# Loading odd and even image rows of the mixing stage as pairs, each pair by one 128-partition DMA

## The chip, the core and the metric

One core of a Trainium2 chip runs the whole kernel in one launch. The metric is the device time in microseconds (us). TensorE (PE), VectorE (DVE), ScalarE (ACT) and GpSimd (POOL) compute; SyncE (SP) issues loads; ACT issues the stores of this stage. All DMAs of the core are carried out by the same 16 DMA engines.

## The reference

Input x is 8 x 64 x 256 x 256 in f32 (batch, channel, row, column). Layer 0 normalizes x by groups, and then, for each batch,

```
y  = mlp1(x)                                   # 64 -> 192 channels, of which 128 are used
x1 = shift1(y[..., :64]);  x2 = shift2(y[..., 64:128])
out = bar0 * x1 + bar1 * x2                    # bar: one softmax weight pair per batch and channel
o  = mlp2(out) * sigmoid(bn(x)) * x
x  = x + o
```

shift1 and shift2 move a quarter of the channels each by one pixel down, up, right or left, with the edge repeated. Everything linear in a batch folds into four 64 x 64 matrices, one for each direction, so the mixing is a sum of four matrix products of shifted images. Layer 1 normalizes again, takes a two-dimensional real FFT, mixes 64 x 32 modes by complex weights, transforms back and adds.

## The kernel before, in words

The kernel runs in stages, one after the other: statistics of x, small matrices from them, the mixing stage (layer 0's output to a scratch tensor in DRAM), a second normalization, the forward transform, the mixing of modes, and the inverse transform. The change lies in the mixing stage and in the last step of the small matrices.

The mixing stage (lines 512 to 742) walks over 8 batches and, in each, over 16 tiles of 16 image rows (`MR`), 128 tiles in all. The loop is unrolled over two batches (`NI` = 32 tiles) and repeated four times. Tile n uses buffer n mod 4 (`NX` = 4) of the input `XT` (mix_x), of `XC` (centred) and of `G` (gated), and buffer n mod 2 of the output `XO` (mix_out) and of psum.

A buffer of `XT` holds, on partitions 0 to 63 (one per channel), the 17 rows from the row above the tile, one column to the right; on partitions 64 to 127, 17 rows from the tile's first row on, without that shift. So one 128-row matrix product reads two shifted images at once, and two such products (m = 0 and 1) make the four directions. Output rows of one parity go to psum partitions 0 to 63 and those of the other to 64 to 127 (`par`).

The steps of one tile, with the lines:

- SP waits until the convolution and the sigmoid of the tile that had the buffer before are done, then issues two loads (L565, L568), each of nine rows by 64 channels to 64 partitions; at the upper and lower image edge there is a third (L572, L574).
- DVE fills the other half of each partition range from the half that was loaded: `up` (L687) copies from the lower to the upper partitions, `down` (L692) from the upper to the lower.
- POOL copies the edge columns (`pad`, L590, two instructions) after `down`.
- PE runs the matrix products (L618) after the pads.
- ACT takes the tile's mean from it (L641) after the pads, in two halves on even tiles; on odd tiles DVE does one half (L700). Then comes the sigmoid (L649).
- DVE multiplies psum by the gate (L722), and then forms the output and its sum (L731).
- ACT issues the store to the scratch (L662) and sums the squares (L667).

Each engine has a written-out order in which work for tile n + 2 (loading step, copies, gate) stands between the steps of tile n; semaphores connect the engines. There is no planner. SP's queue holds nothing but the loads, in the order of the tiles.

In the stage before, DVE writes the folded matrices of all batches into `wall` (L503), four blocks of 64 x 64 per batch as `LAYOUT` says, one instruction for each.

Of the kernel before, what the change touches and what calls it, by code (L numbers as in the profile page):

```python
# [44 lines left out]
LAYOUT = ((0, 0, 2), (1, 0, 1), (0, 1, 0), (1, 1, 3))  # L45
PITCH = W + 1
# [67 lines left out]
def program(nc, x, w1m, b1m, w2m, b2m, sa1, sa2, gamma, beta, wr1, wi1, wr2, wi2, const, out):  # L114
    top = ExitStack()
    with top:
# [34 lines left out]
        wall = sb(top, "wall", [P, B + 1, P])  # L151
# [7 lines left out]
        with ph:  # L159
# [133 lines left out]
            with nc.Block() as block:  # L293
# [77 lines left out]
                def _(dve):  # L371
# [141 lines left out]
        with ph:  # L513
            NX = 4
            XT = [sb(ph, f"mix_x{i}", [P, MR + 1, PITCH]) for i in range(NX)]
# [4 lines left out]
            one = sb(ph, "one", [P, MR + 1])  # L520
            wcur = [sb(ph, f"wcur{i}", [P, P]) for i in range(2)]
            pcur = [sb(ph, f"pcur{i}", [P, 6]) for i in range(2)]
            loaded = [sem(f"mix_loaded{i}") for i in range(NX)]
            stored = [sem(f"mix_stored{i}") for i in range(2)]
            one_set = sem("mix_one_set")
            doubled, padded, batch_ready = sem("mix_doubled"), sem("mix_padded"), sem("mix_batch_ready")
# [4 lines left out]
            ITER = B // 2  # L531

            x1_par = x1.rearrange("b (r e) c w -> b (e c) r w", e=2)

            def split(n):

                return n % 2 == 1

            def loaded_by(i, n):

                q, t = n % NX, n % NB
                edge = 16 if q in (0, NX - 1) else 0
                batch = NB // NX * 32 + edge
                return i * (2 * batch) + n // NB * batch + (t // NX + 1) * 32 + (edge if q == 0 or t == NB - 1 else 0)
# [7 lines left out]
            with nc.Block() as block:  # L552
                @block.sync
                def _(sp):
                    with sp.Fori(0, ITER) as i:
                        for n in range(NI):
                            ch = bass.ds((i * 2 + n // NB) * C, C)
                            t, xt = n % NB, XT[n % NX]


                            sp.wait_ge(conv_done, i * NI + n + 1)
                            sp.wait_ge(sig_done, i * NI + n + 1)
# [8 lines left out]
                            if t == 0:  # L571
                                sp.dma_start(xt[0:C, 0:1, 1:W + 1], x_rows[ch, 0:1, :]).then_inc(loaded[n % NX], 16)  # L572
                            if t == NB - 1:
                                sp.dma_start(xt[C:P, MR:MR + 1, 0:W], x_rows[ch, H - 1:H, :]  # L574
                                             ).then_inc(loaded[n % NX], 16)

                    for k in range(2):
                        sp.wait_ge(stored[k], B * NB // 2 * 16 + 16)

                @block.gpsimd  # L580
                def _(pool):
                    nc.gpsimd.memset(one[:, :], 1.0).then_inc(one_set, 1)
                    pool.wait_ge(one_set, 1)

                    def pad(i, n):

                        pool.wait_ge(doubled, i * NI + n + 1)
                        for half, to, of in ((0, 0, 1), (1, W, W - 1)):
                            h = slice(half * C, (half + 1) * C)
                            last = nc.gpsimd.tensor_tensor(XT[n % NX][h, :, to], XT[n % NX][h, :, of],  # L590
                                                           one[h, :], ALU.mult)
                        last.then_inc(padded, 1)

                    pad(0, 0)
                    pad(0, 1)

                    def body(i, final):
                        for n in range(NI - 2 * final):
                            pad(i, n + 2)

                    iterations(pool, body)

                @block.tensor
                def _(pe):
                    pe.sem_inc(conv_done, NX)
                    with pe.Fori(0, ITER) as i:
                        for n in range(NI):
                            j, k = n // NB, n % 2
# [13 lines left out]
                            last.then_inc(conv_done, 1)  # L622

                @block.scalar
                def _(act):
# [5 lines left out]
                    def gate(i, n):  # L631

                        j = n // NB % 2
                        if n % NB == 0:
                            act.wait_ge(batch_ready, i * 2 + n // NB + 1)
                        act.wait_ge(padded, i * NI + n + 1)

                        act.wait_ge(o_done, i * NI + n + 1)
                        for half in range(1 if split(n) else 2):
                            h = slice(half * C, (half + 1) * C)  # L640
                            last = nc.scalar.activation(  # L641
                                XC[n % NX][h, :].rearrange("p (r w) -> p r w", w=W),
                                XT[n % NX][h, 1:MR:2, 1 - half:1 - half + W],
                                ACT.Identity, bias=pcur[j][h, 4:5])
                        last.then_inc(xc_done, 1)
                        act.wait_ge(xc_done, i * NI + n + 1)
                        if split(n):
                            act.wait_ge(xc_dve, i * NB + n // 2 + 1)
                        nc.scalar.activation(G[n % NX][:, :], XC[n % NX][:, :], ACT.Sigmoid,  # L649
                                             bias=pcur[j][:, 1:2], scale=pcur[j][:, 0:1]).then_inc(sig_done, 1)  # L650
# [22 lines left out]
                def _(dve):  # L673
# [9 lines left out]
                    def up(i, n):  # L683

                        dve.wait_ge(loaded[n % NX], loaded_by(i, n))
                        xt, h = XT[n % NX], MR // 2
                        nc.vector.tensor_copy(xt[C:P, 0:h, 0:W], xt[0:C, 1:h + 1, 1:W + 1])  # L687

                    def down(n):

                        xt, h = XT[n % NX], MR // 2
                        nc.vector.tensor_copy(xt[0:C, h + 1:MR + 1, 1:W + 1], xt[C:P, h:MR, 0:W]).then_inc(doubled, 1)  # L692

                    def centre(i, n):


                        j = n // NB % 2

                        dve.wait_ge(doubled, i * NI + n + 1)
                        nc.vector.tensor_scalar(XC[n % NX][C:P, :].rearrange("p (r w) -> p r w", w=W),  # L700
                                                XT[n % NX][C:P, 1:MR:2, 0:W],
                                                pcur[j][C:P, 4:5], None, ALU.add).then_inc(xc_dve, 1)
# [5 lines left out]
                    for n in range(2):  # L708
                        up(0, n)
                        down(n)  # L710
                    centre(0, 1)

                    def body(i, final):
                        for n in range(NI):
                            j, k = n // NB, n % 2
                            ahead = not (final and n + 2 >= NI)
                            if ahead:
                                up(i, n + 2)
# [6 lines left out]
                            if ahead:  # L725
                                down(n + 2)
# [9 lines left out]
                            if ahead and split(n + 2):  # L736
                                centre(i, n + 2)
# [615 lines left out]
```

## Time and profile before

| | us |
|---|---|
| median of 3 runs | 3149.35 (3144.79 to 3153.17) |
| the profiled execution, its own time | 3155.57 |
| its span in the profile | 3153.8 |

Over the span PE is busy 71%, DVE 64%, ACT 41% and POOL 24%. The stages lie one after another, so these shares are averages over stages with different limits. The mean granted TensorE clock is 0.924 of full speed. A busy time is time in which an engine has an instruction in work; the "DMA share" is the mean busy time of the 16 DMA engines' packets, which overlap a little, so that it can be above 1. "idle before, releaser" in a group says how long the engine waited ahead of it and what ended most of the wait.

### The profile page before, as it was taken

To read this page: it belongs to the slowest core of one execution; us is meant where nothing else is said; L and a number is where in the kernel's file an instruction comes from. 1 tells how busy PE (TensorE), PEld (TensorE's weight loads), DVE (VectorE), ACT (ScalarE), POOL (GpSimd) and SP (SyncE) were. 2 spreads that over 40 slices of the span, in tenths; PEclk is the share of its full clock that TensorE was granted. 3 is DMA by queue.
4 is the path that set the end of the run, shared out by engine and by line. 5 is a ranking of instruction groups with operands and counts; after the bars stand their busy time and mean duration, and the time that the engine had idled before them with its cause. 6 is when DMAs were issued, how large, how long until landed. Compare 5 with 4: busy or idle time off the path is not lost. (4 is left out here: it accounts for less than half of the span.)

```text
span 3153.8 us, 39097 instructions
## 1 busy us (share of the span) xinstructions
PE 2252.6 (71%) x12960; PEld 1081.7 (34%) x12960; DVE 2027.7 (64%) x2317; ACT 1298.2 (41%) x1470; POOL 756.3 (24%) x477
## 2 busy tenths in 40 slices
PE   0000289888989888885999999945554898988784
PEld 0000123223323232331455444425553444444442
DVE  8999689989999999996665565620000454544442
ACT  1111078878887888885332232310000222212220
POOL 1000022332233322332655455500000111111112
PEclk9999999999999999998999999977787999998987
DMA  9999199999999999997877666669998999999999
GB/s 400 429 429 429 36 248 265 271 248 275 270 272 256 270 274 270 269 267 233 316 261 266 241 242 247 232 145 295 304 305 231 384 401 380 394 380 408 389 378 351
DMA packets 537808, 942.87 MB, mean 299 GB/s; under 512 B 16896, under 2 KB 459952, under 8 KB 493136
## 3 DMA queue, kind: packets, MB, share of 16 engines
q1 hardware_dynamic: 299264, 613.33, 61.9%
q10 hardware_dynamic: 202880, 192.95, 20.1%
q0 software_dynamic: 35536, 134.84, 11.2%
q8 instruction: 85, 1.39, 0.2%
q14 instruction: 43, 0.35, 0.0%
HBM read 647.46 MB, written 293.60 MB: 298 GB/s over the span
## 5 line engine op out<-in xcount | busy, mean ns | idle before, releaser
L618 PE MATMUL psum<-mix_x,wcur 128*64 128x512 f32 x4096 | 937.6, 614 | 150.3 <-POOL mix_x L590 134.3
L618 PEld LDWEIGHTS psum<-mix_x,wcur 128*64 128x64 f32 x4096 | 316.6, 139 | 770.8 <-issue 566.4
L1259 PE MATMUL psum<-tab_irow_icol_sign,inv_t 128*128 128x512 f32 x1024 | 495.8, 608 | 18.9 <-DVE inv_x L1306 16.0
L590 POOL TENSOR_TENSOR mix_x<-mix_x,one 64x17 f32<-64x17 f32 x256 | 323.2, 1262 | 747.6 <-DVE mix_x L692 740.2
L641 ACT ACTIVATE centred<-mix_x,pcur 64x2048 f32<-64x2048 f32 x192 | 384.2, 2001 | 204.1 <-POOL mix_x L590 188.9
L1077 POOL TENSOR_TENSOR fwd_diff<-x_tile 128x2048 f32<-128x2048 f32 x64 | 307.9, 4812 | 291.7 <-PE psum L869 256.5
L983 ACT ACTIVATE fwd_rows<-psum 128x512 f32<-128x512 f32 x256 | 152.2, 597 | 412.8 <-PE psum L869 387.9
L263 DVE BATCH_NORM_STATS2 stats<-stat_x 128x512 f32 x512 | 310.0, 678 | 17.5 <-DMA stat_x<-x 14.7
L731 DVE SCALAR_TENSOR_TENSOR mix_out<-gated,centred 128x2048 f32<-128x2048 f32 x128 | 293.6, 2294 | 41.3 <-issue 35.5
L722 DVE SCALAR_TENSOR_TENSOR gated<-psum,pcur,gated 128x2048 f32<-128x2048 f32 x128 | 300.9, 2351 | 16.3 <-PE psum L618 14.4
L1052 DVE COPY fwd_cols<-psum 128x136 f32<-128x136 f32 x512 | 154.6, 394 | 234.2 <-PE psum L880 233.2
L869 PE MATMUL psum<-fwd_sum,tab_ident_frow_fcol 128*64 128x512 f32 x512 | 282.3, 635 | 30.1 <-POOL fwd_diff L1077 20.3
L1287 ACT ACTIVATE inv_t<-psum 128x256 f32<-128x256 f32 x256 | 98.1, 383 | 478.5 <-PE psum L1250 478.5
L1122 PE MATMUL psum<-mode_w,mode_x 128*16 128x64 f32 x4096 | 169.9, 360 | 162.5 <-DMA mode_x<-modes_in 159.8
L869 PE MATMUL psum<-fwd_diff,tab_ident_frow_fcol 128*64 128x512 f32 x512 | 282.7, 636 | 0.0
L649 ACT ACTIVATE gated<-centred,pcur 128x2048 f32<-128x2048 f32 x128 | 268.2, 2095 | 13.3 <-DVE centred L700 5.1
L1306 DVE TENSOR_TENSOR inv_x<-inv_x,psum 128x1024 f32<-128x1024 f32 x128 | 155.6, 1220 | 176.0 <-PE psum L1259 142.0
L1306 DVE TENSOR_TENSOR x_tile<-x_tile,psum 128x1024 f32<-128x1024 f32 x128 | 156.0, 1221 | 168.1 <-PE psum L1259 159.5
L1259 PEld LDWEIGHTS psum<-tab_irow_icol_sign,inv_t 128*128 128x128 f32 x1024 | 199.0, 196 | 167.6 <-issue 149.1
L297 PE MATMUL psum<-s_ones_dmask_spread_npix,w1d 128*64 128x128 f32 x1 | 0.4, 396 | 342.1 <-PEq L200 342.1
L667 ACT ACTIVATE square<-mix_out 128x2048 f32<-128x2048 f32 x128 | 242.5, 1894 | 3.6 <-DVE mix_out L731 3.6
L1250 PE MATMUL psum<-tab_irow_icol_sign,inv_yy 128*128 128x256 f32 x512 | 159.1, 395 | 100.6 <-ACT inv_yy L1281 100.6
(183 smaller groups left out, 1952.5 us busy)
## 6 DMA issues: line engine op xcount, KB each, us to landing
x_tile<-x_scratch SPq DMA_DIRECT2D x184, 1024.0 KB, 7.7
mix_x<-x SPq DMA_DIRECT2D x240, 576.0 KB, 8.2
stat_x<-x SPq DMA_DIRECT2D x64, 2048.0 KB, 14.4
x_scratch<-mix_out ACTq DMA_DIRECT2D x128, 1024.0 KB, 9.1
inv_x<-x_scratch SPq DMA_DIRECT2D x64, 1024.0 KB, 10.9
out<-x_tile POOLq DMA_DIRECT2D x64, 1024.0 KB, 17.0
out<-inv_x POOLq DMA_DIRECT2D x64, 1024.0 KB, 15.6
mode_w<-L_conv_w_imag ACTq DMA_DIRECT2D x16, 2048.0 KB, 21.2
```

The lines of the kernel that those rows point to most:

```text
L263: last = nc.vector.bn_stats(stats[:, bass.ds(b * (NT * 48) + (t * 8 + q) * 6, 6)], XT[t % NX][:, q * 512:(q + 1) * 512])
L590: last = nc.gpsimd.tensor_tensor(XT[n % NX][h, :, to], XT[n % NX][h, :, of], one[h, :], ALU.mult)
L618: last = nc.tensor.matmul(bank(k * 4 + q, 512, C, par * C), wcur[j][:, m * C:(m + 1) * C], XT[n % NX][:, r0:r0 + 3:2, m:m + W], start=(m = ...
L641: last = nc.scalar.activation(XC[n % NX][h, :].rearrange("p (r w) -> p r w", w=W), XT[n % NX][h, 1:MR:2, 1 - half:1 - half + W], ACT.Ident ...
L649: nc.scalar.activation(G[n % NX][:, :], XC[n % NX][:, :], ACT.Sigmoid, bias=pcur[j][:, 1:2], scale=pcur[j][:, 0:1]).then_inc(sig_done, 1)
L667: nc.scalar.activation(SQ[:, :], XO[k][:, :], ACT.Square, accum_out=sqs[:, bass.ds(i * NI + n, 1)]).then_inc(sq_done, 1)
L722: nc.vector.scalar_tensor_tensor(out=G[n % NX][:, :], in0=psum[:, k * SC:(k + 1) * SC], scalar=pcur[j][:, 3:4], in1=G[n % NX][:, :], op0=A ...
L731: nc.vector.scalar_tensor_tensor(out=XO[k][:, :], in0=G[n % NX][:, :], scalar=1.0, in1=XC[n % NX][:, :], op0=ALU.add, op1=ALU.mult, accum_ ...
L869: last = nc.tensor.matmul(bank(n % 2, 512, C, par * C), frow[:, par, :], ED[G0 % 2][par][:, 2 * cp:2 * cp + 2, :], start=True, stop=True)
L1077: nc.gpsimd.tensor_tensor(ED[G0 % 2][1][:, :, :], XW[G0 % NX][:, 0, :, :], XW[G0 % NX][:, 1, :, :], ALU.subtract).then_inc(diff_done, 1)
L1259: last = nc.tensor.matmul(bank(n % 2 * 2 + a), TS[n % 2][:, a * P:(a + 1) * P], icol, start=True, stop=True)
L1306: nc.vector.tensor_tensor(xw, xw, psum[:, n % 2 * 1024:n % 2 * 1024 + 1024] .rearrange("p (a k) -> p a k", a=2), ALU.add).then_inc(added, 1)
```

## The change

The tile's data are laid out by row parity. `XT` becomes 9 slots of 258 columns: slot k holds odd rows (the row 2k - 1 of the tile) on partitions 0 to 63 (`ODD`), shifted by one column, and even rows (2k) on partitions 64 to 127 (`EVEN`). A new buffer `XA` (8 slots of 257 columns) holds the same rows with the column shift the other way round (odd rows without it, even rows with it). For m = 0 the products read `XT`, for m = 1 `XA`, and since the roles of the halves alternate with the output row's parity, there are four blocks of weights instead of two: `LAYOUT` has eight entries and `wall` and `wcur` are twice as wide.

Each slot of `XT` is loaded by a DMA of its own: 128 partitions by 257 columns, from a source pattern of 2 rows x 64 channels x 257 columns that begins one element ahead of the odd row. That makes nine DMAs per tile (eight in the first and the last tile of an image, which have two more of 64 partitions). `XA` is filled by two DVE copies, each within its own partitions. POOL pads with four instructions of 8 or 9 elements, after the load instead of after the copies; ACT's centring waits for the load alone. PE waits for the copies only ahead of its second half. DVE centres a half on 2 tiles of 8 instead of 4 of 8. The function that would load `XA` by DMA is there, but its list of tiles (`A_LOADED`) is empty, so it issues nothing. `wall` is written by 8 instructions over all batches instead of 32.

```diff
-LAYOUT = ((0, 0, 2), (1, 0, 1), (0, 1, 0), (1, 1, 3))
+LAYOUT = ((0, 0, 0), (1, 0, 3), (0, 1, 2), (1, 1, 1),
+          (0, 2, 1), (1, 2, 2), (0, 3, 3), (1, 3, 0))
...
-                    for b in range(B):
-                        for half, slot, d in LAYOUT:
-                            h = slice(half * C, (half + 1) * C)
-                            v.tensor_scalar(wall[h, b, slot * C:(slot + 1) * C], mats[h, b, d, :],
-                                            sm[h, 6, b:b + 1], None, ALU.mult)
+                    for half, slot, d in LAYOUT:
+                        h = slice(half * C, (half + 1) * C)
+                        v.tensor_tensor(wall[h, 0:B, slot * C:(slot + 1) * C], mats[h, :, d, :],
+                                        sm[h, 6, :].unsqueeze(2).to_broadcast([C, B, C]), ALU.mult)
...
-            XT = [sb(ph, f"mix_x{i}", [P, MR + 1, PITCH]) for i in range(NX)]
+            NK = TR // 2
+            XT = [sb(ph, f"mix_x{i}", [P, NK + 1, W + 2]) for i in range(NX)]
+            XA = [sb(ph, f"mix_a{i}", [P, NK, W + 1]) for i in range(NX)]
...
+            ODD, EVEN = slice(0, C), slice(C, P)
+            A_LOADED = ()
+            CENTRE_DVE = (1, 5)
...
+            def row_pair(first, step):
+
+
+                return bass.AP(x.tensor, first, [[C * NPIX, B], [step, 2], [NPIX, C], [1, W + 1]])
...
+                            sp.wait_ge(conv_done, i * NI + n + 1)
+                            sp.wait_ge(sig_done, i * NI + n + 1)
+                            for k in range(t == 0, NK + (t != NB - 1)):
+                                sp.dma_start(xt[:, k, 0:W + 1],
+                                             row_pair((t * TR + 2 * k - 1) * W - 1, W + 1)[bs][0]
+                                             ).then_inc(loaded[q], 16)
...
-                            r0 = t * MR - 1
-                            lo = max(r0, 0)
-                            sp.dma_start(xt[0:C, lo - r0:MR // 2 + 1, 1:W + 1],
-                                         x_rows[ch, lo:r0 + MR // 2 + 1, :]).then_inc(loaded[n % NX], 16)
-                            hi = min(r0 + MR + 2, H)
-                            sp.dma_start(xt[C:P, MR // 2:hi - r0 - 1, 0:W],
-                                         x_rows[ch, r0 + 1 + MR // 2:hi, :]).then_inc(loaded[n % NX], 16)
...
-                        pool.wait_ge(doubled, i * NI + n + 1)
-                        for half, to, of in ((0, 0, 1), (1, W, W - 1)):
...
+                        pool.wait_ge(loaded[n % NX], loaded_by(i, n))
...
+                        for h, to, of in ((ODD, xt[ODD, :, 0], xt[ODD, :, 1]),
+                                          (EVEN, xt[EVEN, :, W], xt[EVEN, :, W - 1]),
+                                          (ODD, xa[ODD, :, W], xt[ODD, 1:NK + 1, W]),
+                                          (EVEN, xa[EVEN, :, 0], xt[EVEN, 0:NK, 0])):
+                            last = nc.gpsimd.tensor_tensor(to, of, one[h, 0:to.shape[1]], ALU.mult)
...
-                                for q in range(4):
+                                if m == 1 and not a_by_dma(n):
+                                    pe.wait_ge(copied, i * len(COPIES) + copies_before(n) + 1)
+                                for q in range(NK // 2):
                                     for par in range(2):
-                                        r0 = 1 - m + par + q * 4
+                                        if m == 0:
+                                            src = xt[:, 2 * q + par:2 * q + par + 2, 1 - par:1 - par + W]
+                                        else:
+                                            src = xa[:, 2 * q:2 * q + 2, par:par + W]
                                         last = nc.tensor.matmul(bank(k * 4 + q, 512, C, par * C),
-                                                                wcur[j][:, m * C:(m + 1) * C],
-                                                                XT[n % NX][:, r0:r0 + 3:2, m:m + W],
-                                                                start=(m == 0), stop=(m == 1))
+                                                                wcur[j][:, (2 * m + par) * C:(2 * m + par + 1) * C],
+                                                                src, start=(m == 0), stop=(m == 1))
...
-                        act.wait_ge(padded, i * NI + n + 1)
+                        act.wait_ge(loaded[n % NX], loaded_by(i, n))
...
+                    rows = (XT[n % NX][EVEN, 0:NK, 0:W], XT[n % NX][ODD, 1:NK + 1, 1:W + 1])[half]
+                    out = XC[n % NX][half * C:(half + 1) * C, :].rearrange("p (r w) -> p r w", w=W)
...
-                        nc.vector.tensor_copy(xt[C:P, 0:h, 0:W], xt[0:C, 1:h + 1, 1:W + 1])
...
-                        nc.vector.tensor_copy(xt[0:C, h + 1:MR + 1, 1:W + 1], xt[C:P, h:MR, 0:W]).then_inc(doubled, 1)
...
+                        if not a_by_dma(n):
+                            nc.vector.tensor_copy(XA[n % NX][ODD, :, 0:W], XT[n % NX][ODD, 1:NK + 1, 1:W + 1])
...
+                        if not a_by_dma(n):
+                            nc.vector.tensor_copy(XA[n % NX][EVEN, :, 1:W + 1], XT[n % NX][EVEN, 0:NK, 0:W]
+                                                  ).then_inc(copied, 1)
```

## Rows read from the trace of the kernel before

**Rows 1.** The page's slices: 40 equal parts of the span, 78.8 us each

```profile
DVE  8999689989999999996665565620000454544442
PEclk9999999999999999998999999977787999998987
DMA  9999199999999999997877666669998999999999
```

**Rows 2.** Busy time by stretch: the mixing stage, and 600 us within it

```profile
388.50:1475.90 1087.40, 937.59 (x4096) 316.64 (x4096) 993.52 (x731) 890.47 (x577) 323.15 (x256) 0.96 1.04 263
600.00:1200.00 600.00, 525.19 (x2303) 177.82 (x2300) 555.06 (x409) 499.10 (x323) 179.76 (x143) 0.97 1.05 267
```

**Rows 3.** Groups by line, 600 to 1200 us

```profile
L618 PE MATMUL psum<-mix_x,wcur 128*64 128x512 f32 x2303 | 526.2, 612 | 76.2 <-POOL mix_x L590 61.6 <-DVE gated L722 7.8 <-issue 6.8
L641 ACT ACTIVATE centred<-mix_x,pcur 64x2048 f32<-64x2048 f32 x108 | 216.1, 2001 | 96.1 <-POOL mix_x L590 88.1 <-issue 7.5
L590 POOL TENSOR_TENSOR mix_x<-mix_x,one 64x17 f32<-64x17 f32 x143 | 181.8, 1271 | 420.8 <-DVE mix_x L692 416.6
L722 DVE SCALAR_TENSOR_TENSOR gated<-psum,pcur,gated 128x2048 f32<-128x2048 f32 x72 | 169.3, 2351 | 8.5 <-PE psum L618 7.6
L731 DVE SCALAR_TENSOR_TENSOR mix_out<-gated,centred 128x2048 f32<-128x2048 f32 x72 | 165.2, 2294 | 24.1 <-issue 20.4 <-DMA x_scratch<-mix_out 2.2
L649 ACT ACTIVATE gated<-centred,pcur 128x2048 f32<-128x2048 f32 x72 | 150.9, 2095 | 6.2 <-DVE centred L700 0.9 <-ACT centred L641 0.4
L667 ACT ACTIVATE square<-mix_out 128x2048 f32<-128x2048 f32 x72 | 136.4, 1894 | 0.0
L692 DVE COPY mix_x<-mix_x 64x2048 f32<-64x2048 f32 x72 | 88.1, 1224 | 2.2
L687 DVE COPY mix_x<-mix_x 64x2048 f32<-64x2048 f32 x71 | 86.7, 1221 | 8.9 <-issue 6.2
L700 DVE TENSOR_SCALAR centred<-mix_x,pcur 64x2048 f32<-64x2048 f32 x36 | 46.3, 1287 | 1.2
L667 ACT ACTIVATION_READ_ACCUMULATOR square<-mix_out x71 | 13.2, 186 | 0.0
L731 DVE DVE_READ_ACCUMULATOR mix_out<-gated,centred x71 | 5.8, 82 | 0.0
```

**Rows 4.** Busy time by stretch: loads alone; loads and stores; the statistics stage

```profile
391.00:400.00 9.00, 0.00 (x0) 0.00 (x0) 2.44 (x2) 0.00 (x0) 0.16 (x1) 0.50 1.12 214
707.00:708.00 1.00, 1.00 (x6) 0.29 (x6) 1.00 (x1) 1.00 (x1) 0.00 (x0) 1.00 1.09 388
10.00:320.00 310.00, 0.00 (x0) 0.00 (x0) 302.37 (x500) 49.20 (x270) 3.51 (x9) 1.00 1.00 425
```

**Rows 5.** Timeline of the start and the end of the stage: start, us, engine, line

```profile
378.37 9.52 DVE L503 TENSOR_SCALAR wall<-psum,sm 64x64 f32<-64x64 f32 x32 [6.82 <-PE psum L353]
388.54 0.75 SPq L565 DMA_DIRECT2D mix_x<-x  x1
389.48 0.61 SPq L568 DMA_DIRECT2D mix_x<-x  x1
...
1459.12 7.11 PE L618 MATMUL psum<-mix_x,wcur 128*64 128x512 f32 x32 [0.17 <-POOL mix_x L590]
...
1475.94 0.82 SPq L754 DMA_DIRECT2D tab_group_ident<-tables  x2
```

**Rows 6.** Timeline of one instruction of the stage before the mixing

```profile
366.93 0.69 DVE L487 TENSOR_TENSOR w2s<-psum,w2t 128x512 f32<-128x512 f32 x1
```

**Rows 7.** Timeline in mid-stage: two load issues, and two pairs of pads

```profile
705.66 0.60 SPq L565 DMA_DIRECT2D mix_x<-x  x1
706.44 0.60 SPq L568 DMA_DIRECT2D mix_x<-x  x1
...
719.21 0.52 POOL L590 TENSOR_TENSOR mix_x<-mix_x,one 64x17 f32<-64x17 f32 x2 [6.19 <-DVE mix_x L692]
...
736.09 3.59 POOL L590 TENSOR_TENSOR mix_x<-mix_x,one 64x17 f32<-64x17 f32 x2 [6.19 <-DVE mix_x L692]
```

**Rows 8.** The page's DMA issues: size, median us from issue to landing

```profile
mix_x<-x SPq DMA_DIRECT2D x240, 576.0 KB, 8.2
```

More of the change, by code:

```diff
@@ L150, in program @@
         params = sb(top, "params", [P, B + 1, 4])
-        wall = sb(top, "wall", [P, B + 1, P])
+        wall = sb(top, "wall", [P, B + 1, 4 * C])
         sums = sb(top, "sums", [P, B * NT])
@@ L531, in program, with a_by_dma, centre_dve, copies_before @@
             ITER = B // 2
-            x1_par = x1.rearrange("b (r e) c w -> b (e c) r w", e=2)
-            def split(n):
-                return n % 2 == 1
+            ODD, EVEN = slice(0, C), slice(C, P)
+            A_LOADED = ()
+            CENTRE_DVE = (1, 5)
+            COPIES = [n for n in range(NI) if n % 8 not in A_LOADED]
+            CENTRES = [n for n in range(NI) if n % 8 in CENTRE_DVE]
+            x1_par = x1.rearrange("b (r e) c w -> b (e c) r w", e=2)
+            def a_by_dma(n):
+                return n % 8 in A_LOADED
+            def centre_dve(n):
+                return n % 8 in CENTRE_DVE
+            def copies_before(n):
+                return sum(m < n for m in COPIES)
+            def centres_before(n):
+                return sum(m < n for m in CENTRES)
             def loaded_by(i, n):
@@ L542, in loaded_by, with a_loaded_by @@
                 edge = 16 if q in (0, NX - 1) else 0
-                batch = NB // NX * 32 + edge
-                return i * (2 * batch) + n // NB * batch + (t // NX + 1) * 32 + (edge if q == 0 or t == NB - 1 else 0)
+                batch = NB // NX * 144 + edge
+                return i * (2 * batch) + n // NB * batch + (t // NX + 1) * 144 + (edge if q == 0 or t == NB - 1 else 0)
+            def a_loaded_by(i, n):
+                mine = [m for m in range(NI) if a_by_dma(m) and m % NX == n % NX]
+                return i * (len(mine) * NK * 16) + (mine.index(n) + 1) * NK * 16
+            def row_pair(first, step):
+                return bass.AP(x.tensor, first, [[C * NPIX, B], [step, 2], [NPIX, C], [1, W + 1]])
             def iterations(engine, body):
@@ L567, in _ @@
[L567 to L575 removed]
+                            load(i, n)
@@ L585, in pad @@
                     def pad(i, n):
-                        pool.wait_ge(doubled, i * NI + n + 1)
-                        for half, to, of in ((0, 0, 1), (1, W, W - 1)):
-                            h = slice(half * C, (half + 1) * C)
-                            last = nc.gpsimd.tensor_tensor(XT[n % NX][h, :, to], XT[n % NX][h, :, of],
-                                                           one[h, :], ALU.mult)
-                        last.then_inc(padded, 1)
[L594 to L601, printed above, removed]
+                        xt, xa = XT[n % NX], XA[n % NX]
+                        pool.wait_ge(loaded[n % NX], loaded_by(i, n))
+                        if a_by_dma(n):
+                            pool.wait_ge(a_loaded[n % NX], a_loaded_by(i, n))
+                        for h, to, of in ((ODD, xt[ODD, :, 0], xt[ODD, :, 1]),
[3 more added lines that the diff above has]
+                            last = nc.gpsimd.tensor_tensor(to, of, one[h, 0:to.shape[1]], ALU.mult)
+                        last.then_inc(padded, 1)
+                    with pool.Fori(0, ITER) as i:
+                        for n in range(NI):
+                            pad(i, n)
                 @block.tensor
@@ L635, in gate @@
                             act.wait_ge(batch_ready, i * 2 + n // NB + 1)
-                        act.wait_ge(padded, i * NI + n + 1)
+                        act.wait_ge(loaded[n % NX], loaded_by(i, n))
                         act.wait_ge(o_done, i * NI + n + 1)
[L639 to L644, printed above, removed]
+                        for half in range(1 if centre_dve(n) else 2):
+                            out, rows = centred(n, half)
+                            last = nc.scalar.activation(out, rows, ACT.Identity,
+                                                        bias=pcur[j][(EVEN, ODD)[half], 4:5])
                         last.then_inc(xc_done, 1)
                         act.wait_ge(xc_done, i * NI + n + 1)
-                        if split(n):
-                            act.wait_ge(xc_dve, i * NB + n // 2 + 1)
+                        if centre_dve(n):
+                            act.wait_ge(xc_dve, i * len(CENTRES) + centres_before(n) + 1)
                         nc.scalar.activation(G[n % NX][:, :], XC[n % NX][:, :], ACT.Sigmoid,
@@ L681, in take, with first, second @@
                                                 -1.0, None, ALU.mult).then_inc(batch_ready, 1)
[L683 removed]
+                    def first(i, n):
                         dve.wait_ge(loaded[n % NX], loaded_by(i, n))
[L686 to L702 removed]
+                        if centre_dve(n):
+                            out, rows = centred(n, 1)
+                            nc.vector.tensor_scalar(out, rows, pcur[n // NB % 2][ODD, 4:5], None,
+                                                    ALU.add).then_inc(xc_dve, 1)
+                        if not a_by_dma(n):
+                            nc.vector.tensor_copy(XA[n % NX][ODD, :, 0:W], XT[n % NX][ODD, 1:NK + 1, 1:W + 1])
+                    def second(n):
+                        if not a_by_dma(n):
+                            nc.vector.tensor_copy(XA[n % NX][EVEN, :, 1:W + 1], XT[n % NX][EVEN, 0:NK, 0:W]
+                                                  ).then_inc(copied, 1)
                     dve.sem_inc(h_done, 2)
@@ L708, in _ @@
                     for n in range(2):
-                        up(0, n)
-                        down(n)
-                    centre(0, 1)
+                        first(0, n)
+                        second(n)
                     def body(i, final):
@@ L725, in body @@
                             if ahead:
-                                down(n + 2)
+                                second(n + 2)
                             dve.wait_ge(h_done, i * NI + 2 + n + 1)
```

35 lines of the change are left out of this document (23 added, 12 removed).

## The prediction

> **What bounds the kernel now.** I read the slices first, to find the stage. Slices 5 to 18, about 390 to 1470 us, are the mixing stage: DVE stands at 9 tenths and so does DMA [rows 1]. The stretches confirm it: the stage takes 1087.4 us, or 8.50 us for each of 128 tiles, and in its middle 600 us hold 72 tiles, 8.33 us each [rows 2, 3]. In those 600 us DVE is busy 555 us, PE 525, ACT 499, POOL 180, and the DMA share is 1.05 at 267 GB/s [rows 2].
>
> Then the groups, for the work of one tile [rows 3]. DVE: 2.351 + 2.294 + 0.082 + 1.221 + 1.224 and half of 1.287 make 7.82 us. ACT: 1.5 centrings of 2.001, then 2.095, 1.894 and 0.186, make 7.18 us. PE: 525 us over 72 tiles make 7.3. DVE is nearest to the period of 8.33 us; it waits most ahead of L731 (24.1 us in 72 tiles) and hardly for a load.
>
> DMA is just as near, which its share alone doesn't tell. When loads run alone, at the stage's start, the share is 1.12 and only 214 GB/s move; with stores beside them 388 GB/s are reached at nearly the same share [rows 4]. So loads to 64 partitions run at half the rate the engines can show. A tile loads 18 rows of 64 channels, 1152 packets of 1024 bytes (two of the DMAs of [rows 8]), and stores 1024 such packets. At 214 GB/s the loads take 1.180 MB / 214 = 5.5 us, at 388 GB/s the stores 1.049 / 388 = 2.7 us: 8.2 us of 8.33. DMA and DVE are both within 7% of the period, and either could take over.
>
> The row fits a rule of the Trainium skill (SBUF — State Buffer, Door 1: the DMA port swizzle): partitions 0 to 63 reach only 8 of 16 ports, so that such a transfer has about half the bandwidth. By that rule alone the change would free some 2.5 us of DMA per tile, and the sum would be that of the first rival below.
>
> **The change, part by part.**
>
> *Loads.* Removed: two DMAs per tile. Added: nine DMAs of 128 descriptors of 1028 bytes, eight in the two edge tiles of an image: 14 x 9 + 2 x 8 = 142 per batch, 1136 in all, and two small edge DMAs beside each of the 16 edge tiles (at most 2 x 64 packets, 0.3 us per edge tile, not counted). Bytes hardly change (1.18 MB per tile). What changes is the shape. Every load of before has the same outermost count on both sides, 64 channels on 64 partitions. The new destination has 128 partitions, but the source is written as 2 rows x 64 channels x 257 columns, with row and channel steps that can't merge into one. If the hardware shares a DMA among its engines by cutting both patterns at their outermost dimension, the source can be cut only in two, and each row-pair DMA runs on two engines, 64 descriptors on each. No row of before shows a DMA with such a source, so the number of engines is unknown from both sides: sixteen (a gain) and two (a large loss). I take two, since a split of a pattern with outermost count 2 into more than two equal parts would need a second dimension to be cut.
>
> The Trainium skill states this as a rule (DMA: Bandwidth & Descriptors, Why a DMA increments its semaphore by 16 and not by 1): the engines used are the largest number up to 16 that divides the slowest dimension of both patterns, and on SP's queue the lowest-numbered ones. No run here shows it so far; by it the same two engines would carry all of them. My high chance for this case hangs on that sentence.
>
> With two engines, these have 1136 x 64 = 72,704 load packets each. Time of one packet on one engine: from below, the statistics stage moves 425 GB/s on 16 engines, 1028 bytes in 38.7 ns; the best stretch of mixed 1 KB packets, 388 GB/s, gives 42.2 ns; from above, loads alone, 214 GB/s, give 76.6 ns [rows 4]. The port limit, if it is one, would not bind two engines, so the value lies near 42; but the odd rows' packets start four bytes ahead of a kilobyte boundary and every packet is four bytes over, which no packet of before is. I take 50 ns. The stores stay on all engines: 128 tiles x 64 packets = 8192 on each, at 42.2 ns.
>
> The same page's section How a descriptor splits into AXI transactions would charge 40 beats instead of 32 for the misaligned packet, 42.2 x 40 / 32 = 53 ns, an estimate from that page; the sum would be 218 us higher.
>
> Sum of the stage: 72,704 x 0.050 = 3635, 8192 x 0.0422 = 346, in all 3981 us in which the two engines have no gap, since SP runs up to four tiles ahead. That is 31.1 us per tile. Around it: about 2 us until the first packet moves, and after the last landing the last tile's work. Before, from the last convolution's start to the stage's end are 1475.94 - 1459.12 = 16.8 us [rows 5]. To this I add 3 us for the copies and pads, and 7 for TensorE, whose clock stood at 0.50 (1.2 GHz) at the start of the stage after it had idled [rows 4], which doubles its 7.11 us. That gives 27. The stage: 3981 + 2 + 27 = 4010 us against 1087.4.
>
> *All that runs on engines* is covered by 31 us per tile: DVE needs 7.5, ACT 7.7, PE 7.3 or 15 at the low clock, POOL four pads. If that cover is gone, this is what it costs. Copies: the same two of 64 x 2048. They now stay in their lanes; L700, in lane, takes 1.287 and the crossing copies 1.224 [rows 3], so nothing either way, within 0.1 us. Centring: DVE does a quarter of a tile's count instead of a half, 7.82 - 0.32 = 7.50 us; ACT takes it, 7.18 + 0.50 = 7.68 us. Its even half now crosses partitions, at the same price by the copies' rows. Pads: four instead of two. A pair took 0.52 us beside an idle DVE and 3.59 beside a busy one [rows 7]; the mean is 1.27 for one. Four cost 5.1 us, between 1.0 and 7.2. They start at the landing and no longer behind `down`, so the 76 us of PE's waits in 600 [rows 3] may shrink. PE's new wait for the copies holds up only its own second half; DVE's `second` waits for nothing new. Weights: a load goes with every matmul already, so four blocks cost nothing.
>
> *SP's queue.* Two issues stand 0.78 us apart [rows 7], 0.94 at the start [rows 5]. Nine make 7.0 to 8.5 us per tile. Only loads are queued there, and 31 us cover it.
>
> *wall.* 32 instructions in 9.52 us [rows 5] become 8 of 64 x 512 out of PSUM. The nearest is L487 at 0.69 [rows 6]: 5.5 us, 4.0 saved on the path. Bounds: none saved, to 6.
>
> **The sum.** Profiled execution 3155.6 - 1087.4 + 4010 - 4 = 6074 us. That execution is 6.2 us above the median of the runs, so 6068, say 6070.
>
> **The rivals.**
>
> 1. *All 16 engines carry each pair.* Then the loads fall to 1.18 MB / 388 GB/s = 3.1 us per tile, DMA to 5.8, and the highest of the others sets the pace: ACT at 7.68, DVE 7.50, PE 7.3, SP 7.0. DVE now has 0.51 us per tile beside its work (8.33 - 7.82). With 0.2 to 0.3 beside ACT's 7.68 the period is 7.9 to 8.0, and 128 x 0.4 = 51 us go, with `wall` 55: 3149 - 55 = 3094 us, within 3050 to 3130. For it: the half rate of the loads in [rows 4], which it cures. Against: the source's outermost count of 2. This is the rival on the other side.
> 2. *Sixteen engines, but SP's or POOL's queue becomes the pace.* Nine issues at 0.94 us are 8.5 us per tile, above 8.33: 128 x 0.17 = 22 us more, 4 less by `wall`, 3167 us. It decides from 0.92 us per issue on. POOL would need 2.1 us for a pad, more than any row shows.
> 3. *Two engines, but at the rate of the loads of before*, 76.6 ns: 5569 + 346 + 29 = 5944 us for the stage, 8008 us in all. For it: no faster stretch of pure loads is in the trace. Against: a doubling beside stores at the same share [rows 4] speaks for a limit that lies behind the engines.
>
> **How the numbers follow.** Two engines: 0.85, of which 0.03 for rival 3 (packet of over 70 ns) and 0.82 for the forecast. Rival 1: 0.10. Rival 2: 0.05. For the forecast, 38.7 ns give 2814 + 346 + 29 = 3189 us, 5246 in all; 66 ns give 4798 + 375 = 5173 and 7231. I take 5350 to 7300 as the range; it leaves out rivals 1 and 2 (0.15), rival 3, and the ends: 2 in 10. What a measurement tells from no change is 0.3%, 9 us. Slower: 0.85 and half of rival 2's 0.05, 0.87; faster: rival 1 and a little, 0.11; same 0.02.
>
> **What would show it.** Right: 128 row-pair packets of 1028 bytes per DMA with a DMA share of about 0.2 (two engines full, the others with the stores only) throughout the stage, 65 to 80 GB/s, some 31 us per tile, DVE waiting at its first copy and ACT at its centring for mix_x<-x, PE's clock at 0.5 for most of the stage, and landings far above 8.2 us. Wrong: a share near 0.7 to 1.0 and DVE or ACT at 9 tenths (rival 1), or SP's queue without a gap between issues and loads landing in 3 us (rival 2). The packet's time is read from the stage's length: each ns of it is 73 us.

## The result, and the profile after

The changed kernel takes 5681.32 us (median of 4 runs, 5679.03 to 5689.05) against 3151.26; the ratio is 1.8018, interval 1.7981 to 1.8054. The profiled execution spans 5681.1 us. The mixing stage, from its first load to the next stage's first load, grew from 1087.4 us [rows 2] to 4003.11 - 383.80 = 3619.3.

```profile
383.80 17.05 SPq L593 DMA_DIRECT2D mix_x<-x  x8
...
4003.11 0.83 SPq L788 DMA_DIRECT2D tab_group_ident<-tables  x2
```

The page's slices, 142 us each, answer to [rows 1]:

```profile
DVE  8952222222222222222222222222565530044443
PEclk9986666666666666666666666666899987799998
DMA  9922222222222222222222222222676769999999
```

In the stage DVE fell from 9 tenths to 2, and so did DMA. The kernel no longer runs short of an engine, nor of all DMA engines together. The stretches say the same, and give the rate of loads alone, which was 214 GB/s [rows 4] and is 47. As in [rows 2], a line gives the stretch and its length, then the busy time (and instructions) of PE, of its weight loads, of DVE, ACT and POOL, and last the granted TensorE clock, the DMA share and GB/s:

```profile
600.00:1200.00 600.00, 196.68 (x676) 63.63 (x678) 159.33 (x120) 164.99 (x103) 45.20 (x88) 0.65 0.23 79
391.00:400.00 9.00, 0.00 (x0) 0.00 (x0) 0.00 (x0) 0.00 (x0) 0.00 (x0) 0.50 0.14 47
```

A share of 0.14 with loads alone is that of two engines in sixteen, with the little overlap that made 1.12 of a full share before. Through the stage the share of 0.23 and the 79 GB/s are what the prediction named as its signs (about 0.2, 65 to 80 GB/s).

The page's groups answer to [rows 3]: ACT's centring and DVE's copy take the same time per instruction as before, and ACT, DVE and POOL wait for the load.

```profile
L685 ACT ACTIVATE centred<-mix_x,pcur 64x2048 f32<-64x2048 f32 x224 | 448.1, 2000 | 2355.4 <-DMA mix_x<-x 2338.4
L733 DVE COPY mix_a<-mix_x 64x2048 f32<-64x2048 f32 x128 | 156.3, 1221 | 1952.6 <-DMA mix_x<-x 1951.6
L629 POOL TENSOR_TENSOR mix_x<-mix_x,one 64x9 f32<-64x9 f32 x256 | 180.3, 704 | 3317.6 <-DMA mix_x<-x 3310.1
```

How many engines carry a row pair can be counted. The page counts short packets; first the kernel before, then the changed one:

```profile
DMA packets 537808, 942.87 MB, mean 299 GB/s; under 512 B 16896, under 2 KB 459952, under 8 KB 493136
```

```profile
DMA packets 536281, 943.78 MB, mean 166 GB/s; under 512 B 15328, under 2 KB 458384, under 8 KB 491568
mix_x<-x SPq DMA_DIRECT2D x1136, 128.5 KB
```

The only load stream that differs is this stage's: 272 DMAs before; 1136 row pairs and 32 edge DMAs after. If each engine that takes part in a DMA leaves one short packet, the DMAs that moved no row pair keep 16896 - 272 x 16 + 32 x 16 = 13056, and the row pairs have 15328 - 13056 = 2272 = 2 x 1136. That is two each, to the packet. What the count assumes, one short packet per engine, is borne out by the other runs below: with sixteen engines for each of 2272 and of 272 loads it gives 49408 and 16896, and both were counted.

The timeline gives the period of one tile, 1532.99 - 1505.23 = 27.76 us, and of four, (1622.74 - 1508.74) / 4 = 28.5 us each:

```profile
1505.23 1.22 DVE L733 COPY mix_a<-mix_x 64x2048 f32<-64x2048 f32 x1 [20.98 <-DMA mix_x<-x]
1508.74 1.22 DVE L738 COPY mix_a<-mix_x 64x2048 f32<-64x2048 f32 x1
1508.86 5.53 PE L656 MATMUL psum<-mix_x,wcur 128*64 128x512 f32 x16 [18.71 <-DVE gated L758]
1514.21 3.62 PE L656 MATMUL psum<-mix_a,wcur 128*64 128x512 f32 x16
...
1532.99 1.22 DVE L733 COPY mix_a<-mix_x 64x2048 f32<-64x2048 f32 x1 [20.69 <-DMA mix_x<-x]
...
1622.74 1.22 DVE L738 COPY mix_a<-mix_x 64x2048 f32<-64x2048 f32 x1
```

An engine that carries row pairs has 9 x 64 load packets in such a tile and 64 of the store. With 2.70 us for the stores, as predicted, a load packet takes (27.76 - 2.70) / 576 = 43.5 ns. The loads alone agree: 2 x 1028 bytes at 47 GB/s are 43.7 ns. But 27.76 us is one of the shorter tiles. By the prediction's own sum over the whole stage, (3619.3 - 346 - 29) / 72,704, a load packet costs 44.6 ns.

### The profile page after: what moved, and what is told of

It is laid out like the page before. It is cut to its first block and busy times, and to the rows that moved or that the text cites. A ratio compares the mean times of both kernels' runs of the same rounds, so it can differ in the third digit from the quotient of the medians.

```text
span 5681.1 us, 41943 instructions
## 1 busy us (share of the span) xinstructions
PE 2497.0 (44%) x12960; PEld 1147.8 (20%) x12960; DVE 1973.2 (35%) x2261; ACT 1381.5 (24%) x1502; POOL 700.1 (12%) x733
## 2 busy tenths in 40 slices
DMA packets 536281, 943.78 MB, mean 166 GB/s; under 512 B 15328, under 2 KB 458384, under 8 KB 491568
## 5 line engine op out<-in xcount | busy, mean ns | idle before, releaser
L656 PE MATMUL psum<-mix_x,wcur 128*64 128x512 f32 x2048 | 742.8, 892 | 2432.6 <-DVE gated L758 2378.9
L685 ACT ACTIVATE centred<-mix_x,pcur 64x2048 f32<-64x2048 f32 x224 | 448.1, 2000 | 2355.4 <-DMA mix_x<-x 2338.4
L733 DVE COPY mix_a<-mix_x 64x2048 f32<-64x2048 f32 x128 | 156.3, 1221 | 1952.6 <-DMA mix_x<-x 1951.6
L656 PEld LDWEIGHTS psum<-mix_x,wcur 128*64 128x64 f32 x2048 | 223.4, 206 | 2946.8 <-issue 2891.9
L629 POOL TENSOR_TENSOR mix_x<-mix_x,one 64x9 f32<-64x9 f32 x256 | 180.3, 704 | 3317.6 <-DMA mix_x<-x 3310.1
L656 PE MATMUL psum<-mix_a,wcur 128*64 128x512 f32 x2048 | 463.1, 592 | 0.0
L730 DVE TENSOR_SCALAR centred<-mix_x,pcur 64x2048 f32<-64x2048 f32 x32 | 42.4, 1326 | 710.2 <-DMA mix_x<-x 710.2
L656 PEld LDWEIGHTS psum<-mix_a,wcur 128*64 128x64 f32 x2048 | 158.2, 136 | 286.5 <-issue 286.5
```

The lines of the kernel that those rows point to most:

```text
L629: last = nc.gpsimd.tensor_tensor(to, of, one[h, 0:to.shape[1]], ALU.mult)
L656: last = nc.tensor.matmul(bank(k * 4 + q, 512, C, par * C), wcur[j][:, (2 * m + par) * C:(2 * m + par + 1) * C], src, start=(m == 0), stop ...
L685: last = nc.scalar.activation(out, rows, ACT.Identity, bias=pcur[j][(EVEN, ODD)[half], 4:5])
```

## The experiments

Each ran beside the kernel before (medians 3151 to 3153 us).

**Two DMAs per tile, by parity.** The rows of one parity are one DMA with 64 channels outermost; a tile at an image edge has one more DMA instead of two. Everything else is the changed kernel (`even_rows` is written like `odd_rows`).

```diff
+            def odd_rows(b, t):
...
+                k0 = int(t == 0)
+                rows = bass.AP(x.tensor, (t * TR + 2 * k0 - 1) * W - 1,
+                               [[C * NPIX, B], [NPIX, C], [2 * W, NK + 1 - k0], [1, W + 1]])[b][0]
+                return slice(k0, NK + 1), slice(0, W + 1), rows
...
-                            for k in range(t == 0, NK + (t != NB - 1)):
-                                sp.dma_start(xt[:, k, 0:W + 1],
-                                             row_pair((t * TR + 2 * k - 1) * W - 1, W + 1)[bs][0]
-                                             ).then_inc(loaded[q], 16)
...
+                            k, w, rows = odd_rows(bs, t)
+                            sp.dma_start(xt[0:64, k, w], rows).then_inc(loaded[q], 16)
...
+                            k, w, rows = even_rows(bs, t)
+                            sp.dma_start(xt[64:128, k, w], rows).then_inc(loaded[q], 16)
```

> The changed kernel with its layout and all its engine work, but the rows of a tile loaded by two DMAs, one for the odd rows (64 partitions x 9 rows x 257 columns) and one for the even rows, both from SP. Packets, bytes and alignment are those of the changed kernel (1028 bytes, the odd ones beginning four bytes ahead of a row); the outermost count is 64 on both sides. Theory (the row-pair source, outermost count 2, confines a DMA to two engines): all 16 engines carry the loads again; DMA per tile is 1.18 MB at 214 GB/s + 1.05 MB at 388 GB/s = 8.2 us, the stage 1050 to 1090 us and the kernel 3110 to 3155 us. Rival A (the misaligned 1028-byte packets are what is slow): still above 5000 us. Rival B (the price was in the number of DMAs, nine each of which must finish): also back to about 3130 us, so this run does not tell it from the theory; e2 does.

Measured: 3053.82 us (3048.97 to 3057.47), ratio to the kernel before 0.9682 (0.9658 to 0.9705). That is below the theory's range, and far from rival A: with the same bytes, packets and alignment the loss is gone, and 3.2% are gained. The short packets are again 16896 for 272 loads, sixteen for each. Its stretches:

```profile
600.00:1200.00 600.00, 558.29 (x2518) 204.07 (x2514) 571.66 (x424) 587.48 (x373) 121.40 (x316) 0.99 1.09 294
390.00:396.00 6.00, 0.00 (x0) 0.00 (x0) 2.48 (x2) 2.61 (x2) 2.47 (x3) 0.50 1.13 204
```

**The same, each DMA cut into 62 and 2 channels.** `rows[0:62]` and `rows[62:64]` of the odd and of the even rows, each to its partitions.

> As e1_by_parity, but each of the two DMAs cut by channel into one of 62 partitions and one of 2. No row pair is left, there are four DMAs per tile instead of nine, and the larger has 558 packets. Theory: 62 = 2 x 31 and 2 have no divisor from 3 to 16 that could be an engine count other than 2, so every DMA again runs on two engines: 576 load packets on each of the two per tile at 43.5 ns + 64 store packets, 27.7 us per tile, about 5680 us in all with a DMA share of 0.23. Rival B (nine small DMAs per tile, their issue or their completion): four DMAs of which two are large, so at most about 3200 us. Rival A (misalignment): as e1, above 5000 us in both.

Measured: 5697.25 us, one run. The loss is back with four DMAs per tile and no row pair in them. The short packets are 13824, again two for each of the 512 cut DMAs: 16896 - 4352 + 16 x 16 + 512 x 2. What this kernel and the changed one share is the divisor: of 62 on both sides, of 2 on both sides, and of 2 against 128, the largest common divisor up to 16 is 2. Rival B falls.

**The same with aligned packets**, 256 columns from the row's start instead of 257.

> As e2_62_and_2 (two engines for every load), but 256 columns instead of 257, so that each packet has 1024 bytes and begins at a row's start. If the prediction's surcharge for misaligned packets exists, the two engines go faster: from 43.5 ns per load packet toward the 42.2 of the kernel before's best stretch, 576 x 1.3 ns = 0.7 us per tile, about 5600 us. If a packet costs the same however it lies, 5690 within 15 us.

Measured: 5673.19 us, one run, 17 us below the 5690 of "costs the same", 2 more than it allowed, and far above the 5600 of a surcharge. Its tiles are 1532.85 - 1505.33 = 27.52 us apart, against 1536.58 - 1508.92 = 27.66 in the kernel with 257 columns: 0.2 ns for each packet, or 0.3 by the whole times (24 us over 72,704). Half of those packets, the odd rows', began four bytes ahead of a row, so one such packet costs at most some 0.6 ns. So alignment costs next to nothing.

**Eighteen DMAs of 64 partitions per tile**, each pair's odd and even row by itself:

```diff
                             for k in range(t == 0, NK + (t != NB - 1)):
-                                sp.dma_start(xt[:, k, 0:W + 1],
-                                             row_pair((t * TR + 2 * k - 1) * W - 1, W + 1)[bs][0]
-                                             ).then_inc(loaded[q], 16)
+                                pair = row_pair((t * TR + 2 * k - 1) * W - 1, W + 1)[bs][0]
+                                for half, h in enumerate((ODD, EVEN)):
+                                    sp.dma_start(xt[h, k, 0:W + 1], pair[half]).then_inc(loaded[q], 16)
```

> The changed kernel, but each row pair loaded by two DMAs of 64 partitions (odd row, even row) instead of one of 128: 18 DMAs per tile, each with the outermost count 64, the packets unchanged. Theory: 16 engines carry each, so DMA work per tile is again below 8 us; what is left is SP's queue, 18 issues at 0.78 us = 14.0 us per tile, 128 x 14.0 + 35 = 1830 us for the stage, 3890 us in all, within 3750 to 4400 if an issue costs up to 1.0 us. Rival B (the change is slow because a tile's load is many small DMAs): twice as many must then be slower than the changed kernel, above 5681 us.

Measured: 3797.56 us, one run, 1884 below the changed kernel with twice its DMAs. SP's queue is now without a gap, and DMA is half idle (share 0.56):

```profile
699.88 45.11 SPq L595 DMA_DIRECT2D mix_x<-x  x62
600.00:1200.00 600.00, 401.83 (x1440) 134.54 (x1438) 329.35 (x245) 340.87 (x214) 92.56 (x180) 0.82 0.56 168
```

That is 0.73 us per issue, 13.1 per tile, and the issues are the pace. The short packets are 49408 = 13056 + 2272 x 16: sixteen engines for each.

**The even rows' load on ACT's queue**, for tile n + 4 after the store of tile n, in the layout by parity; and the same for the upper-half load of the kernel before. `load_even` issues the DMA from ACT.

```diff
+                            if not (final and n + NX >= NI):
+                                load_even(i * 2 + (n + NX) // NB, (n + NX) % NB, n % NX)
```

> As e1_by_parity, but the even rows' DMA (partitions 64 to 127) is issued by ACT, one tile ahead of SP's order by nature of its place after the store of tile n, for tile n + 4. Both halves of the partitions can then be filled at the same time. Theory P (a load to 64 partitions is limited on the side of the SBUF, by the half of the partitions it reaches; 214 GB/s): the two queues interleave, loads run near 380 GB/s, DMA falls to about 5.9 us per tile, ACT at 7.7 us and DVE at 7.5 set the pace, period 7.9 to 8.0, kernel 3070 to 3110 us. Rival Q (1 KB reads from DRAM are limited to 214 GB/s whatever their partitions): as e1_by_parity within 10 us, 3110 to 3155.

> The kernel before, with only its upper-half load (rows 9 to 17, partitions 64 to 127) moved from SP to ACT's queue, after the store of tile n, for tile n + 4. Nothing else is changed. Theory P: DMA per tile falls from 8.2 to about 5.9 us; DVE at 7.82 us remains, with what it waits for: period 8.1 to 8.3, kernel 3100 to 3145 us. Rival Q: no change, 3140 to 3160.

Measured: 3228.2 us (ratio 1.0234, 1.0209 to 1.0259) and 3383.65 us (1.0729, 1.0702 to 1.0756). Both theories missed the time. But the rate of loads alone, at the start of the first of the two, decides between P and Q:

```profile
390.00:396.00 6.00, 1.13 (x4) 0.52 (x6) 3.15 (x3) 4.00 (x3) 3.25 (x6) 0.50 1.09 341
702.00:703.00 1.00, 0.32 (x2) 0.23 (x4) 0.97 (x2) 1.00 (x1) 0.00 (x0) 1.00 0.00 0
```

The same packets run at 341 GB/s when both halves of the partitions are filled at once, and at 204 when one after the other. Rival Q falls. The run changed two things, though: both halves are filled at once, and there are two queues. That one queue could be what holds the loads to 204 GB/s is answered by the kernel before: SP's queue alone carried 425 GB/s in the statistics stage [rows 4], and from 2200 to 2300 us it carried 33206 packets, 332 per us, where 204 GB/s are 204 per us (1223 in 6 us). Its line for those 100 us, with packets, MB and share of the 16 engines' time:

```profile
q1 hardware_dynamic: 33206, 16.92, 64.7%
```

So theory P holds, as far as these runs can tell; no run loads 1 KB packets to all 128 partitions from one queue and on all engines.

In mid-stage nothing of the higher rate is left. The second row above is a microsecond in which DMA stands idle. Such gaps are few, and the 600 us as a whole still move only 246 GB/s against 294 at a share near 1:

```profile
600.00:1200.00 600.00, 496.93 (x2106) 181.55 (x2108) 484.08 (x360) 494.59 (x312) 153.22 (x264) 0.94 1.01 246
699.05 1.22 DVE L755 COPY mix_a<-mix_x 64x2048 f32<-64x2048 f32 x1 [2.05 <-DMA mix_x<-x]
699.26 4.02 ACT L692 ACTIVATE centred<-mix_x,pcur 64x2048 f32<-64x2048 f32 x2 [5.78 <-issue]
703.31 2.09 ACT L698 ACTIVATE gated<-centred,pcur 128x2048 f32<-128x2048 f32 x1
704.09 0.66 ACTq L707 DMA_DIRECT2D mix_x<-x  x1
```

The load stands in ACT's order behind a centring, a gate and the store. DVE then waits for loads: 65.4 us ahead of L755 in 600 us, and 45.6 ahead of its centring, where the layout by parity on SP alone had none. Whether that is the place in ACT's order, or that the load now shares a queue with the store and runs beside SP's, these runs don't separate; an earlier place wasn't tried. Why both kernels became slower stays open.

**Pads behind the copies again**, in the layout by parity: POOL waits for `copied`, ACT's centring for `padded`.

```diff
-                        pool.wait_ge(loaded[n % NX], loaded_by(i, n))
+                        pool.wait_ge(copied, i * len(COPIES) + copies_before(n) + 1)
...
-                        act.wait_ge(loaded[n % NX], loaded_by(i, n))
+                        act.wait_ge(padded, i * NI + n + 1)
```

> As e1_by_parity, but POOL's pads wait for the copies and ACT's centring for the pads, as in the kernel before; loads, layout, weights and shares of work are those of e1. If the 99 us between e1 and the kernel before come from the freed pads and centring, this is back near 3130 to 3150 us; if they come from DVE's lighter share of centring, it stays within 15 us of e1.

Measured: 3174.31 us (10 runs, 3158.23 to 3180.26), ratio 1.0054 (1.0034 to 1.0075), above the 3130 to 3150 expected. The whole gain of the layout by parity is gone with two waits; which of the two does more wasn't tried. From 600 to 1200 us DVE waits ahead of L778 again (38.4 + 11.0 us), and PE and ACT wait for the pads, as before. A line gives us in total, times, longest:

```profile
PE psum L667 <- POOL mix_a L640: 64.0, 36, 5.8
ACT centred L696 <- POOL mix_a L640: 57.6, 29, 9.9
DVE mix_out L778 <- issue: 38.4, 37, 1.8
```

**Other shares of the centring**, `CENTRE_DVE = (1, 3, 5, 7)` and `(1, 4, 6)` in the layout by parity:

> As e1_by_parity (3054 us), but DVE centres a half on 4 tiles of 8 again, as the kernel before. Theory E (with all engines on the loads the pace is the busier of ACT and DVE): ACT falls to 7.1 us per tile, DVE rises by 0.32 to 7.5 us and takes over with some waits: period 7.8 to 7.9, kernel 3080 to 3095 us. Rival F (the pace of e1 is the landing of the loads, 9.3 us after issue and used as soon as they land): no change, 3054 within 10 us.

> As e1_by_parity, but DVE centres a half on 3 tiles of 8 (1, 4, 6). Theory E: ACT 7.31 us, DVE 7.38 us per tile, period 7.45 to 7.55, kernel 3035 to 3050 us. Rival F: no change from e1.

Measured: 3076.34 us (ratio 0.9748, 0.9711 to 0.9785) and 3056.41 us (0.9685, 0.9648 to 0.9721). Half on DVE costs 22 us against a quarter, a little less than theory E said, and rival F, no change, falls. Three eighths bring nothing: theory E's 3035 to 3050 is missed by 6 us, and by itself this run can't tell E from F. A reading that fits both: with a quarter ACT was busy 587 of 600 us, and taking work from it helps no more once DVE is level (586 of 600 with three eighths).

The first of these runs also has the same share of centring on DVE as the kernel before, and is still 75 us faster. So of the gain of 99 us, the lighter share explains 22 at most.

**The second buffer loaded on 1 and on 2 tiles of 8**, with half of the centring on DVE:

> As e7_parity_centre_4of8 (3076 us), but on tile 3 of 8 the second buffer is loaded by two more DMAs (8 rows by 64 partitions each) and DVE's two copies fall away there. Theory E: DVE 7.54 - 0.31 = 7.23 us per tile, ACT 7.07, PE 7.1: period 7.4 to 7.55, kernel 3025 to 3050 us, below e1. Rival F (the landing of the loads is the pace already): the added 1 MB per eight tiles makes it later, 3060 to 3100 us.

> As e11, with the second buffer loaded on tiles 3 and 7 of 8. Theory E: DVE 6.93, ACT 7.07, PE 7.1 us per tile, period 7.3 to 7.5, 3010 to 3045 us. Rival F: 3080 to 3150 us, since DMA then moves 2.5 MB per tile.

Measured: 3053.45 us (ratio 0.9679, 0.965 to 0.9708) and 3042.65 us (0.9646, 0.9616 to 0.9676). The first misses theory E's range by 3 us; the second lies in it, and it is the fastest version here, 109 us below the kernel before and 34 below the same kernel without these loads. Both are below rival F's ranges. The stretch of the second:

```profile
600.00:1200.00 600.00, 567.30 (x2568) 208.73 (x2566) 564.33 (x416) 563.50 (x362) 199.77 (x316) 0.99 1.10 333
```

PE, DVE and ACT are level at 94%, and DMA moves 333 GB/s at a share of 1.10.

## Why the prediction was right, point by point

- *Two engines per row pair.* Shown in three ways: by the count of short packets, by the cut into 62 and 2 channels, which loses as much in another shape, and by the return of the time when the outermost count is 64. The rule of the Trainium skill that the forecast's chance hung on (DMA: Bandwidth & Descriptors, Why a DMA increments its semaphore by 16 and not by 1) agrees with the trace: two for 2 and for 62, sixteen for 64. That the two are the lowest-numbered engines, no view here shows.
- *The packet.* The term that was mis-sized: 50 ns were taken, 43.5 measured in one tile and 44.6 over the whole stage. The surcharge had been put down to misalignment, and the aligned kernel shows that there is hardly any (0.2 to 0.3 ns). By the tile's 43.5 ns, the loads were set 72,704 x 6.5 ns = 473 us too high and the rest of the stage 82 us too low, so the total came out 3619 us against 4010. Those 82 us are for the most part the longer tiles: 28.5 us on average over four, where 27.76 was the one read. The Trainium skill's account of misaligned packets (DMA: Bandwidth & Descriptors, How a descriptor splits into AXI transactions), from which the prediction worked out its estimate of 53 ns, is not borne out by the trace.
- *The row read as loads and stores.* The stretch of 388 GB/s in [rows 4] was taken for loads with stores beside them. All its packets are on ACT's queue, q10, so they are stores alone, from all 128 partitions. The view of the queues from 707 to 708 us has one line (packets, MB, share of the 16 engines' time):

```profile
q10 hardware_dynamic: 379, 0.39, 109.3%
```

  So 42.2 ns is the price of a store packet, which is what the sum used it for, and the 2.7 us for a tile's stores stand. But it didn't show that loads double beside stores, which was the argument against rival 3.
- *That rate against the limit of a half.* Loads alone rose from 204 to 341 GB/s when both halves of the partitions were filled at once. This agrees with the Trainium skill's rule on partitions 0 to 63 (SBUF — State Buffer, Door 1: the DMA port swizzle), by which a load to one half of the partitions runs at about half the rate. Rival 3 wanted 76.6 ns for a packet on two engines; 43.7 were measured with loads alone, so it fell.
- *DMA as near to the bound as DVE.* Wrong. I had added the loads' time alone and the stores' time alone, 5.5 + 2.7 us. They overlap: by that sum the layout by parity would need 1.18 MB / 204 GB/s + 2.7 = 8.5 us per tile, and its 79 tiles in 600 us took 7.6. It moves 294 GB/s with loads that alone still run at 204, and the fastest version 333. The DMA share was 1.05, 1.09 and 1.10. A share near 1 said that the engines always had packets, not that they could do no more.
- *What bounded the kernel before.* I put 0.51 us per tile beside DVE's work and left them there. In the layout by parity they are the chain DVE copy, pad, product and centring: two waits put back cost 120 us. That the same chain made them in the kernel before is argued from its waits for the pads [rows 3]; the waits weren't taken out there. Rival 1 counted 0.2 to 0.3 of them as staying and so came to 3094 us, within 3050 to 3130; sixteen engines with all else of the change gave 3054.
- *The covered parts.* Copies 1.221 and 1.224 us as before, within the partitions now and across them then; centring 2.000. The pads of a tile take 1.51 + 0.47 us in mid-stage, 2.05 in the mean, against 5.1 predicted. `wall` took 5.60 us instead of 9.52, 3.9 saved of the predicted 4.0.
- *SP's queue.* 0.73 us an issue, 0.78 predicted. Rival 2, nine issues on sixteen engines, wasn't built; eighteen gave the pace that the same working predicts.
- *TensorE's clock.* The granted clock was 0.65 of full speed on average, not 0.5 for most of the stage. PE idles until DVE frees psum, and DVE's gate stands behind the copy that waits for the load. The tile's first half then takes 5.53 us and its second 3.62, the latter at full speed (32 products took 7.11 before [rows 5]). At 9.2 of 27.8 us it stayed covered.

## What to carry to other kernels

Look at the outermost count of both patterns of a DMA before you look at its bytes: a count of 2 on the source's side, or of 62 on both, left 14 of 16 engines out of the loads and cost a factor of 1.8. A stage's DMA share near 1 doesn't prove that DMA bounds it; compare the GB/s that the same share carries elsewhere. And an idle half microsecond per tile on the busiest engine can be a chain of waits that a weaker condition removes: here that was worth 120 us, where shifting the centring was worth 22 and loading part of the second buffer 34.

## What the runs showed that I had not expected

- Loads that alone run at 204 GB/s don't cap a mixed stage: 294 to 333 GB/s with stores beside them, at the same share.
- Moving one of two loads to another issuing engine slowed both kernels, by 2.3 and 7.3%, although it raised the rate of loads alone, in the first of them to 341 GB/s.
- Packets of 1028 bytes, half of them beginning four bytes ahead of a row, cost on average within 0.3 ns of aligned ones of 1024.
